# A two-layer gated cross-attention kernel: three instruction blocks are joined into one

## The chip, the cores and the metric

The kernel runs on one core of a Trainium2 chip. A core has five engines with an instruction stream each: TensorE (PE in the profile, with its weight loads as PEld), VectorE (DVE), ScalarE (ACT), GpSimd (POOL) and SyncE (SP), and 16 DMA engines that they share. Engines meet only through semaphores. The metric is the time of one execution in microseconds of device time, taken as the median of several runs.

## The reference, cut to what matters

```python
x = x + tanh(g_xattn[0]) * L0_xattn(layernorm(x), ctx)   # correlation attention: top 13 delays
x = x + tanh(g_ffn[0])   * L0_ffn(layernorm(x))          # 8 experts, 2 per token, and a shared one
x = x + tanh(g_xattn[1]) * L1_xattn(layernorm(x), ctx, mask)   # 16 heads over 77 keys
x = x + tanh(g_ffn[1])   * L1_ffn(layernorm(x))          # 32 experts, 4 per token, and a shared one
```

x has 4 x 1024 rows of 256 float32 numbers, ctx has 4 x 77 rows. In layer 0's feed-forward part each row goes to 2 of 8 experts; in layer 1's to 4 of 32. The products of layer 0 and of layer 1's attention are made of three matmuls each on values split into a high and a low part.

## The kernel before, in words

The 4096 rows of x stay in SBUF (`x`, 32 tiles of 128 rows, or 8 chunks of 4 tiles). The program is written by hand engine by engine: each engine has its own list of instructions with its own waits, and nothing reorders them. It comes in three blocks, one behind the other, and each holds a list for each of the five engines:

- **Folds** (first block, L307 to L675). The context is multiplied into the weights of both attentions (`wqk1` and `vwo1` are the folded weights of layer 1, two heads at a time, and SP stores them to `wqk_d` and `vwo_d`), layer 0's attention scores give the 13 delays, and the first chunk is normalised for the feed-forward part. Its last instructions are ACT's `fold_heads(7)` (L461), PE's transposes of chunk 0 (`transposes_job`, L225) and SP's stores of the last two heads (L334).
- **Layer 0** (second block, L842 to L1555). First the dense part: for each of 8 chunks the router, the shared expert and the attention of the chunks to come. Then 39 blocks of 256 rows that are gathered by expert: SP loads a block's rows (`rows<-slots_d`), PE, ACT and DVE compute, POOL scatters the result to `y0_d` with two indirect DMAs (L999). Beside them the folded weights of layer 1 are split into high and low parts and stored again. ACT opens the block with `wr_hi` (L1015) and the eviction of the transposed chunk 0 (`x_hi`, L1013); DVE follows with `x_lo` (L1153), and PE's first matmul there, the router of chunk 0 (L1399), needs that.
- **Layer 1** (third block, L1759 to L2331). SP first loads the two expert results of the first four tiles from `y0_d` (`first_rows`, L1765, into the end of `xbT`); DVE adds them to x and takes the statistics (`mv_a`), POOL makes 1/sqrt(var + eps) of them (`rstd`, L1834 to L1844), ACT normalises (`xa`, L1913), PE transposes, ACT and DVE evict (`xa_hi`, L1908, and `xa_lo`, L2024), and the first scores follow (L2191). From there on attention, routing and dispatch run as a pipeline over the 32 tiles, then the 32 experts, then the sums.

Between two blocks every engine runs a drain (it waits until what it has issued is done) and the five meet in a barrier: SP, ACT, DVE and PE report to POOL, and POOL releases them. In the profile these instructions carry the line of the block that they end: L307, L842 and L1759.

At the end of layer 0's list, POOL waits until all its scatters have landed, one semaphore for each of six groups of blocks (L1003 and L1004), and SP waits until the last parts of the split weights are stored and the cleared tables written (L918, L919). In layer 1's `first()`, POOL makes its constants (`xa`'s column of ones, `tri`, `allone`, `cum`, `rows`, `outrow`, `ones1`, `full`: L1847 to L1863); DVE and PE wait for all eight of them by the semaphore `c3` before `xa_lo` of tile 0 and before the first scores.

Of the kernel before, what the change touches and what calls it, by code (L numbers as in the profile page):

```python
# [7 lines left out]
ALU = mybir.AluOpType  # L8
ACT = mybir.ActivationFunctionType
AX = mybir.AxisListType  # L10
# [7 lines left out]
S = 77  # L18
# [82 lines left out]
def build(nc, io):  # L101
    root = ExitStack()
    with root:
# [143 lines left out]
        with one:  # L247
# [59 lines left out]
            with nc.Block() as block:  # L307
                @block.sync
                def _(sp):
                    def load_x(c):  # L310
                        sp.dma_start(x[:, c * CT:(c + 1) * CT, :], x_v[:, c * CT:(c + 1) * CT, :]).then_inc(x_in[c], 16)

                    def load_heads(m):

                        want(sp, f1_mm, 8 * (m - NH + 1))
                        cols = slice(m * P, (m + 1) * P)
                        for w, src in ((wk1, "wk1"), (wv1, "wv1")):
                            sp.dma_start(w[:, m % NH, :, :], io[src].rearrange("(k p) n -> p k n", p=P)[:, :, cols])\
                               .then_inc(w1_in[m % NH], 16)
                        for w, src in ((wqT1, "wqT1"), (wo1, "wo1")):  # L320
                            sp.dma_start(w[:, m % NH, :], io[src][cols, :]).then_inc(w1_in[m % NH], 16)

                    def store_heads(m):

                        sp.wait_ge(f1_out, 8 * m + 4)
                        if m == 0:
                            sp.wait_ge(mask_row, 64)
                        for b in range(B):
                            sp.dma_start(wqk_d[b].rearrange("(k p) n -> p k n", p=P)[:, :, 2 * m * S:2 * (m + 1) * S],
                                          wqk1[:, m % 2, :, b, :]).then_inc(qk1_stored[m % 2], 16)  # L330
                        sp.wait_ge(f1_out, 8 * m + 8)
                        for hh in range(2):
                            h = 2 * m + hh
                            sp.dma_start(vwo_d[:, h * S:(h + 1) * S, :].rearrange("b s n -> s b n"),  # L334
                                          vwo1[:, m % 2, hh, :, :]).then_inc(vo1_stored[m % 2], 16)

                    for name, dst in (("ctxT", ctxT), ("wk0", wk0), ("wqT0", wqT0)):
                        sp.dma_start(dst[:], io[name].rearrange("(k p) n -> p k n", p=P)).then_inc(w0_in, 16)
                    sp.dma_start(bias0[:], io["bias0"].rearrange("p (a k) -> p a k", a=3)).then_inc(w0_in, 16)
                    load_x(0)  # L340
                    load_x(1)
                    for name, dst in (("wv0", wv0), ("wo0", wo0)):
                        sp.dma_start(dst[:], io[name].rearrange("(k p) n -> p k n", p=P)).then_inc(bo_in, 16)
                    for c in range(2, CHUNKS):
                        load_x(c)
                    for b in range(B):
                        sp.dma_start(vwo0[S:S + 1, b, :], io["bo0"].rearrange("(a n) -> a n", a=1)).then_inc(bo_in, 16)
                    sp.dma_start(htab[:], io["htab"].rearrange("(c p) n -> p c n", p=P)).then_inc(htab_in, 16)
                    sp.dma_start(mask_u[:], io["mask"].rearrange("b s -> (b s)").rearrange("(a n) -> a n", a=1))\
                      .then_inc(mask_in, 16)  # L350
                    for m in range(NH):
                        load_heads(m)
                    sp.dma_start(wgu0[:], io["wgu0"].rearrange("(k p) n -> p k n", p=P)[:, :, E0 * 2 * P:])\
                      .then_inc(ffn0_w_in, 16)
                    sp.dma_start(wd0[:], io["wd0"].rearrange("(u p) n -> p u n", p=P)[:, E0:, :]).then_inc(ffn0_w_in, 16)
                    sp.dma_start(wr0[:], io["wr0"].rearrange("(k p) n -> p k n", p=P)).then_inc(ffn0_w_in, 16)
                    sp.wait_ge(mask_ready, 1)
                    for par in range(2):
                        for hh in range(2):
                            sp.dma_start(wqk1[P - 1:P, par, KD - 1, :, hh * S:(hh + 1) * S], mask_f[:]).then_inc(mask_row, 16)  # L360
                    for c in range(CHUNKS):

                        b, half = c // 2, c % 2
                        sp.wait_ge(s_out, c + 1)
                        for copy in range(2):
                            sp.dma_start(st_d[b, :, copy * L + half * CHUNK:copy * L + (half + 1) * CHUNK],
                                         sT[:, half, :]).then_inc(s_stored[half], 16)
                        if half:

                            for par in range(2):  # L370
                                sp.wait_ge(s_stored[par], 32 * (b + 1))
                            want(sp, uv_mm, b - 1)
                            for sign in range(2):
                                shift = bass.AP(st_d.tensor, b * S * 2 * L + (S - 1 if sign == 0 else L - S + 1),
                                                [[2 * L - 1 if sign == 0 else 2 * L + 1, S], [1, L]])
                                sp.dma_start(skew[:, b % 2, sign, :], shift).then_inc(skew_in[b % 2], 16)
                    for m in range(CHUNKS):
                        if m + NH < CHUNKS:
                            load_heads(m + NH)
                        store_heads(m)  # L380
                        if m == 2:
                            sp.wait_ge(w_ready, 2)
                            sp.dma_start(w_d, wrow[:]).then_inc(w_stored, 16)
                        if m == 3:
                            sp.wait_ge(mt_ones, 1)
                            sp.wait_ge(w_stored, 16)
                            shifted_job(sp, 0)
                            shifted_job(sp, 1)
                    sp.wait_ge(ffn0_w_in, 48)

                @block.gpsimd
                def _(pool):
                    pool.memset(ident[:], 0.0).then_inc(ident_zero, 1)
                    pool.memset(neghalf[:], -0.5).then_inc(consts_ready, 1)
                    pool.memset(signs[:, 0:3], 1.0).then_inc(consts_ready, 1)
                    pool.memset(signs[:, 3:4], -1.0).then_inc(consts_ready, 1)
                    pool.wait_ge(ident_zero, 1)
                    pool.affine_select(out=ident[:], in_=ident[:], compare_op=ALU.not_equal, fill=1.0, base=0,
                                       pattern=[[-1, P]], channel_multiplier=1).then_inc(ident_ready, 1)
                    pool.wait_ge(consts_ready, 3)  # L400

                    def last_column(m):

                        pool.wait_ge(w1_in[m % NH], 64 * (m // NH + 1))
                        pool.tensor_scalar(wqT1[:, m % NH, 0:D - 1], wqT1[:, m % NH, 0:D - 1], wqT1[:, m % NH, D - 1:D], None,  # L405
                                           ALU.subtract).then_inc(wq_ready, 1)

                    for c in range(CHUNKS):
                        ln_rstd_job(pool, c, c % 2)
                        if c == 1:  # L410
                            pool.wait_ge(mask_in, 16)
                            pool.tensor_scalar(mask_f[:].rearrange("p b s -> p (b s)"), mask_u[:], MASKED, None, ALU.mult)\
                                .then_inc(mask_ready, 1)
                    for m in range(CHUNKS):
                        last_column(m)
                        if m == CHUNKS - 2:
                            ln_rstd_job(pool, QB, 0)

                @block.scalar
                def _(act):  # L420
                    act.dma_start(gates[:, 0:2], bass.AP(io["g_xattn"].tensor, 0, [[0, P], [1, 2]])).then_inc(gates_in, 16)
                    act.dma_start(gates[:, 2:4], bass.AP(io["g_ffn"].tensor, 0, [[0, P], [1, 2]])).then_inc(gates_in, 16)
                    act.wait_ge(gates_in, 32)
                    act.activation(tg[:], gates[:], ACT.Tanh).then_inc(tg_ready, 1)
# [1959 lines left out]
```

## Time and profile before

| what | us |
|---|---|
| median of 3 runs | 1023.62 |
| lowest and highest run | 1015.46, 1024.27 |
| the profiled execution | 1024.65 |
| its span, first to last instruction | 1022.6 |

The profiled execution is 1.03 us above the median. Of its time 2.05 us lie outside the span. TensorE's granted clock was 0.926 of full speed on average. In the rows below times are microseconds from the span's start unless they are marked ns, and a name such as SPq or POOLq is an engine's sequencer: it shows instructions that don't reach the engine itself (waits, branches, drains, the issue of DMAs).

### The profile page before, as it was taken

What the parts mean: (1) busy time and instruction counts of PE and PEld (TensorE: products, weight loads), DVE (VectorE), ACT (ScalarE), POOL (GpSimd) and SP (SyncE); (2) the same over time, 40 slices, a digit from 0 to 9 for tenths busy, and PEclk for the clock granted to TensorE, in tenths of its full rate; (3) what the DMA queues carried; (4) which work ended last, traced back from release to release, by engine and by line L of the source; (5) the groups of instructions that cost most, each with busy time, mean ns of one, the idle gap of its engine ahead of it and who ended that gap; (6) DMA issues with size and microseconds to landing.
All of it is one profiled execution on the core that took longest, in us unless ns stands there. A gap on an engine that the chain in (4) does not pass through costs nothing. (4 is left out here: it accounts for less than half of the span.)

```text
span 1022.6 us, 18469 instructions
## 1 busy us (share of the span) xinstructions
PE 879.8 (86%) x5433; PEld 744.1 (73%) x5433; DVE 632.6 (62%) x2000; ACT 501.4 (49%) x1813; POOL 564.0 (55%) x635
## 2 busy tenths in 40 slices
PE   4998777999999979889199899999999978999940
PEld 3564446888888779889188889899898857888720
DVE  4603114688778857557278889999999843444441
ACT  1321654444544246546086778878878822222200
POOL 1400113466666727557448777767777653877851
PEclk8987997899999989999699999999999979999975
DMA  9630788367987888996499924514444205899687
GB/s 305 218 100 0 226 240 203 92 204 223 277 260 221 283 260 276 316 332 225 150 165 257 226 94 180 178 58 140 121 153 140 64 12 149 155 224 250 73 211 159
DMA packets 157812, 189.70 MB, mean 186 GB/s; under 512 B 16035, under 2 KB 137017, under 8 KB 157714
## 3 DMA queue, kind: packets, MB, share of 16 engines
q1 hardware_dynamic: 109810, 121.87, 39.9%
q0 software_dynamic: 30720, 46.46, 20.8%
q10 hardware_dynamic: 17184, 20.19, 5.8%
q8 instruction: 46, 0.75, 0.3%
q14 instruction: 52, 0.43, 0.1%
HBM read 96.19 MB, written 103.63 MB: 195 GB/s over the span
## 5 line engine op out<-in xcount | busy, mean ns | idle before, releaser
L1938 ACT ACTIVATE att<-bank,mx 128x77 f32<-128x77 f32 x512 | 159.0, 343 | 1.0 <-DVE mx L2019 0.9
L1879 POOL DMA_INDIRECT slots_d<-rows,place x128 | 131.4, 1027 | 36.4 <-issue 35.5
L1938 ACT ACTIVATION_READ_ACCUMULATOR att<-bank,mx 128x1 f32 x512 | 115.6, 226 | 0.0
L999 POOL DMA_INDIRECT y_d<-rows x78 | 77.3, 991 | 62.3 <-DVE rows L1377 34.7
L959 POOL DMA_INDIRECT slots_d<-rows,place x64 | 65.2, 1019 | 19.0 <-issue 19.0
L1399 PE MATMUL bank<-wd_hi,act_hi 128*128 128x256 f32 (+1 forms) x206 | 66.5, 323 | 1.3 <-DVE act_lo L1372 0.7
L1893 POOL DMA_INDIRECT acc_d<-expert_out,target_rows x32 | 49.6, 1550 | 26.8 <-issue 23.1
L953 POOL TENSOR_TENSOR act_lo<-prod,act_hi 128x512 fp32r<-128x512 f32 x28 | 36.8, 1313 | 39.9 <-ACT act_hi L1035 39.8
L2019 DVE TENSOR_REDUCE mx<-bank 128x6 f32<-128x462 f32 (+1 forms) x96 | 55.1, 573 | 5.6 <-PE bank L2193 4.9
L1401 PE MATMUL bank<-wd_hi,act_lo 128*128 128x256 f32 (+1 forms) x206 | 58.4, 284 | 0.0
L1400 PE MATMUL bank<-wd_lo,act_hi 128*128 128x256 f32 (+1 forms) x206 | 58.3, 283 | 0.0
L1893 POOL DMA_INDIRECT result<-expert_out,target_rows x32 | 49.5, 1546 | 14.3 <-issue 8.5
L2034 DVE TENSOR_TENSOR attT_lo<-bank,attT_hi 128x512 fp32r<-128x512 f32 (+2 forms) x128 | 55.6, 475 | 1.3 <-ACT attT_hi L1928 0.7
L1399 PE MATMUL bank<-x_hi,first_scores 128*128 128x512 f32 x128 | 53.3, 416 | 0.0
L2046 DVE TENSOR_TENSOR att<-att,den 128x924 f32<-128x924 f32 x64 | 51.2, 800 | 2.2
L1400 PE MATMUL bank<-x_lo,first_scores 128*128 128x512 f32 x128 | 52.0, 406 | 0.0
L1401 PE MATMUL bank<-x_hi,first_scores 128*128 128x512 f32 x128 | 52.0, 406 | 0.0
L1925 ACT ACTIVATE attT_hi<-bank 128x512 fp32r<-128x512 f32 x64 | 38.8, 608 | 25.4 <-PE bank L2230 25.4
L2230 PE MATMUL bank<-ident,att 128*128 128x128 f32 x320 | 51.0, 274 | 0.0
L405 POOL TENSOR_SCALAR wqT<-wqT 128x255 f32<-128x255 f32 x8 | 7.5, 941 | 78.0 <-DMA wo<-in_wo 77.9
L1399 PE MATMUL bank<-wgu_hi,x_hi 128*128 x156 | 48.1, 308 | 1.7 <-issue 1.7
L1979 ACT ACTIVATE expert_silu<-bank 128x256 f32<-128x256 f32 x32 | 12.3, 383 | 73.4 <-PE bank L2307 73.4
(318 smaller groups left out, 3009.9 us busy)
## 6 DMA issues: line engine op xcount, KB each, us to landing
rows<-slots_d SPq DMA_DIRECT2D x39, 260.0 KB, 4.3
slots_d<-zrow SPq DMA_DIRECT2D x8, 1168.0 KB, 10.8
expert_rows<-slots_d SPq DMA_DIRECT2D x32, 292.0 KB, 3.7
expert_gate_up<-in_wgu SPq DMA_DIRECT2D x28, 256.0 KB, 4.1
x_res<-y_d POOLq DMA_DIRECT2D x14, 512.0 KB
wqk_d<-wqk SPq DMA_DIRECT2D x32, 154.0 KB, 3.5
vwo_d<-vwo SPq DMA_DIRECT2D x16, 308.0 KB
x_res<-in_x SPq DMA_DIRECT2D x8, 512.0 KB, 8.5
```

What stands on the lines that cost most here:

```text
L959: pool.indirect_dma_start(slots0_d, bass.IndirectOffsetOnAxis(ap=place0[:, c % 3, i:i + 1], axis=0), rows_of(c)[:, i, :], None, bounds_che ...
L999: pool.indirect_dma_start(y0_d, bass.IndirectOffsetOnAxis(ap=x_rows(s)[:, b, D:D + 1].bitcast(I32), axis=0), y_rows(s, b), None, bounds_ch ...
L1399: pe.matmul(to, a_hi, b_hi, start=start, stop=False)
L1400: pe.matmul(to, a_hi, b_lo, start=False, stop=False)
L1401: return pe.matmul(to, a_lo, b_hi, start=False, stop=stop)
L1879: pool.indirect_dma_start(slots_d, bass.IndirectOffsetOnAxis(ap=place[:, n % 3, k:k + 1], axis=0), rows[:, n % 3, :], None, bounds_check=S ...
L1893: pool.indirect_dma_start(total, bass.IndirectOffsetOnAxis(ap=target[:, e % NY, b:b + 1], axis=0), y[:, e % NY, b, :], None, bounds_check= ...
L1938: last = act.activation(att[:, par, h * S:(h + 1) * S], bank[:, a, i * S:(i + 1) * S], ACT.Exp, scale=-1.0, bias=mx[:, par, h:h + 1], accu ...
L2019: dve.tensor_reduce(mx[:, par, h:h + count], e, AX.X, ALU.min).then_inc(mx_ready, 1)
L2034: last = dve.tensor_tensor(attT_lo[0:p1, cols], bank[0:p1, 3 + g % 2, at:at + w * P], attT_hi[0:p1, cols].bitcast(F32), ALU.subtract)
L2046: return dve.tensor_tensor(heads, heads, over, ALU.mult)
L2230: last = pe.transpose(bank[0:w, 3 + g % 2, (j % 4) * P:(j % 4 + 1) * P], att[:, par, j * P:j * P + w], ident[:])
```

## The change

The lists of the first two blocks become functions (`folds_sync`, `layer0_sync`, `folds_gpsimd` and so on), and each engine's list in the third block calls the two of its own before its old content. There is one block instead of three, so the two drains and barriers in between are gone. No instruction of an engine is reordered but for one: in POOL's `first()`, the norm of tile 0 (`rstd("a", 0, 0)`) comes behind the constants. And one wait is added: at the end of layer 0, SP waits for the six scatter semaphores itself, as POOL does.

```diff
-            with nc.Block() as block:
-                @block.sync
-                def _(sp):
+            def folds_sync(sp):
...
-                @block.gpsimd
-                def _(pool):
+            def folds_gpsimd(pool):
...
-            with nc.Block() as block:
-                @block.sync
-                def _(sp):
+            def layer0_sync(sp):
...
+                for g in range(6):
+                    sp.wait_ge(scattered[g], scat_end[g])
                 for par in range(2):
                     sp.wait_ge(part_out[par], POUT + 32 * dmas(PIECES - 2 + par))
                 sp.wait_ge(cleared, 16 * (2 * CHUNKS + 1 + E0))
...
                 @block.sync
                 def _(sp):
+                    folds_sync(sp)
+                    layer0_sync(sp)
+
                     y0_v = y0_d.rearrange("(n p k) d -> p n k d", p=P, k=K0)
...
                     def first():
                         pool.memset(xa[:, :, D - 1:D], 1.0).then_inc(c3, 1)
-                        rstd("a", 0, 0)
                         pool.memset(tri[:], 1.0).then_inc(c3_zero, 1)
...
                         pool.affine_select(out=tri[:], in_=tri[:], compare_op=ALU.not_equal, fill=float(CHOSEN), base=0,
                                            pattern=[[1, P]], channel_multiplier=-1).then_inc(c3, 1)
+                        rstd("a", 0, 0)
```

The same two calls are put at the head of the lists of POOL, ACT, DVE and PE.

At the first joint, ACT's list before, from the last folded heads to the first evictions of layer 0:

```order
L461 ACTIVATE vwo<-bank,tanh_gates 77x512 [waits fold1_mm] x4
L307 UNCONDITIONAL_BRANCH
L1006 UNCONDITIONAL_BRANCH [waits barrier_Pool_Activation_PE_DVE_SP_release]
L1015 ACTIVATE wr_hi<-wr 128x20
L1013 ACTIVATE x_hi<-bank 128x512 [waits ln_T]
L1013 ACTIVATE x_hi<-bank 128x512
```

And now:

```order
L457 ACTIVATE vwo<-bank,tanh_gates 77x512 [waits fold1_mm] x4
L1007 ACTIVATE wr_hi<-wr 128x20
L1005 ACTIVATE x_hi<-bank 128x512 [waits ln_T]
L1005 ACTIVATE x_hi<-bank 128x512
```

The wait for the barrier is gone; what is left is the wait for PE's transposes (`ln_T`).

At the second joint, SP's list before, from the last part of the split weights (`wd<-vwo_d`) to the first loads of layer 1:

```order
L853 DMA wd<-vwo_d 80x256
L842 UNCONDITIONAL_BRANCH [waits cleared,s_stored1,s_stored0]
L1760 UNCONDITIONAL_BRANCH [waits barrier_Pool_Activation_PE_DVE_SP_release]
L1765 DMA xbT<-y_d 128x512 x4
L1770 DMA even_values<-vwo_hi_d 128x9x256
```

And now (`s_stored0` and `s_stored1` are the semaphores of the stored parts; `rows_moved0` to `rows_moved3`, `experts_added0` and `experts_added1` are those of the scatters):

```order
L845 DMA wd<-vwo_d 80x256
L1758 DMA xbT<-y_d 128x512 [waits experts_added1,experts_added0,s_stored0,rows_moved3,s_stored1,rows_moved2,cleared,rows_moved1,rows_moved0]
L1758 DMA xbT<-y_d 128x512 x3
L1763 DMA even_values<-vwo_hi_d 128x9x256
```

The first load waits for the scatters themselves and no longer for POOL's release.

POOL's list at the same joint, before:

```order
L842 UNCONDITIONAL_BRANCH [waits rows_moved3,experts_added0,rows_moved2,experts_added1,rows_moved1,rows_moved0]
L1822 UNCONDITIONAL_BRANCH [waits barrier_Pool_Activation_PE_DVE_SP_gather]
L1847 MEMSET xa 128x2
L1837 TENSOR_SCALAR veps_a<-mv_a 128x1 [waits a_stats]
L1839 TENSOR_TENSOR rstd_a<-veps_a,neghalf 128x1 [waits a_eps]
L1843 TENSOR_SCALAR shift_a<-rstd_a,mv_a 128x1 [waits z_ready]
L1849 MEMSET tri 128x128
...
L1862 AFFINE_SELECT tri<-tri 128x128 [waits consts3_zero]
L1837 TENSOR_SCALAR veps_a<-mv_a 128x1 [waits a_stats]
```

And now:

```order
L1843 MEMSET xa 128x2 [waits rows_moved3,experts_added0,rows_moved2,experts_added1,rows_moved1,rows_moved0]
L1844 MEMSET tri 128x128
...
L1857 AFFINE_SELECT tri<-tri 128x128 [waits consts3_zero]
L1833 TENSOR_SCALAR veps_a<-mv_a 128x1 [waits a_stats]
L1835 TENSOR_TENSOR rstd_a<-veps_a,neghalf 128x1 [waits a_eps]
L1839 TENSOR_SCALAR shift_a<-rstd_a,mv_a 128x1 [waits z_ready]
L1833 TENSOR_SCALAR veps_a<-mv_a 128x1 [waits a_stats]
```

The constants stand ahead of the wait for the first statistics, and the norms of tiles 0 and 1 follow each other.

## Rows read from the trace of the kernel before

**Rows 1.** The page's first line.
```profile
span 1022.6 us, 18469 instructions
```

**Rows 2.** Timeline, first joint: start, length, engine, line, instruction, idle before.
```profile
153.04 2.65 ACT L461 ACTIVATE vwo<-bank,tanh_gates 77x512 f32<-77x512 f32 x4 [1.44 <-PE bank L624]
...
155.72 0.77 SPq L334 DMA_DIRECT2D vwo_d<-vwo  x2
...
156.98 0.22 ACT L1015 ACTIVATE wr_hi<-wr 128x20 fp32r<-128x20 f32 x1 [1.29 <-PEq L307]
...
158.21 1.29 DVE L1153 TENSOR_TENSOR x_lo<-bank,x_hi 128x512 fp32r<-128x512 f32 x2 [0.79 <-ACT x_hi L1013]
...
159.64 0.34 PE L1399 MATMUL bank<-wr_hi,x_hi 128*128 128x10 f32 x1 [4.22 <-DVE x_lo L1153]
```

**Rows 3.** Line L307: ns min/median/max, first and last start.
```profile
L307 POOLq DRAIN x1: 2137/2137/2137, 143.8 to 143.8; - x1
...
L307 ACTq EVENT_SEMAPHORE  x1: 17/17/17, 156.9 to 156.9; - x1
```

**Rows 4.** Windows: us, busy time (instructions) by engine, PE clock, DMA share, GB/s.
```profile
160.00:162.00 2.00, 2.00 (x11) 2.00 (x11) 2.00 (x1) 1.98 (x2) 1.00 (x1) 0.50 0.35 86
...
168.00:170.00 2.00, 1.15 (x7) 0.67 (x5) 1.17 (x4) 0.48 (x3) 0.00 (x0) 1.00 1.17 237
...
208.00:234.00 26.00, 25.65 (x157) 22.05 (x157) 20.78 (x67) 13.20 (x25) 17.95 (x18) 1.00 0.68 212
...
312.00:338.00 26.00, 24.71 (x162) 21.51 (x160) 20.25 (x74) 10.87 (x19) 19.53 (x19) 1.00 0.86 254
```

**Rows 5.** Waits of PE from 330 to 495: total us, times, longest.
```profile
PE bank L1506 <- DMA rows<-slots_d: 10.0, 4, 4.8
```

**Rows 6.** Lines L1004 and L842, the second joint on the sequencers.
```profile
L1004 POOLq EVENT_SEMAPHORE  x3: 17/43/5492, 491.0 to 491.1; - x3
...
L842 SPq COMPARE_BRANCH  x1: 41/41/41, 490.5 to 490.5; - x1
...
L842 POOLq COMPARE_BRANCH  x1: 41/41/41, 496.7 to 496.7; - x1
L842 POOLq DRAIN  x1: 3823/3823/3823, 496.8 to 496.8; - x1
L842 SPq EVENT_SEMAPHORE  x1: 17/17/17, 500.8 to 500.8; - x1
```

**Rows 7.** Timeline behind the second joint.
```profile
500.92 1.76 SPq L1765 DMA_DIRECT2D xbT<-y_d  x4
...
506.22 0.31 POOL L1837 TENSOR_SCALAR veps_a<-mv_a 128x1 f32<-128x1 f32 x1 [5.21 <-DVE mv_a L2011]
...
507.65 0.20 POOL L1849 MEMSET tri<- 128x128 bf16 x1
...
509.12 0.38 ACT L1908 ACTIVATE xa_hi<-bank 128x256 fp32r<-128x256 f32 x1 [0.78 <-PE bank L2199]
...
509.55 0.29 POOL L1862 TENSOR_SCALAR_AFFINE_SELECT tri<-tri 128x128 bf16<-128x128 bf16 x1
509.88 0.42 DVE L2024 TENSOR_TENSOR xa_lo<-bank,xa_hi 128x256 fp32r<-128x256 f32 x1 [2.30 <-POOL tri L1862]
```

**Rows 8.** Line L1759, POOL's drain at the program's end.
```profile
L1759 POOLq COMPARE_BRANCH  x1: 46/46/46, 1018.3 to 1018.3; - x1
L1759 POOLq DRAIN  x1: 3902/3902/3902, 1018.5 to 1018.5; - x1
```

**Rows 9.** Timeline, POOL's last DMA and its last operation in the folds.
```profile
144.85 1.00 POOL L405 TENSOR_SCALAR wqT<-wqT 128x255 f32<-128x255 f32 x1
...
1003.26 0.86 POOL L1900 DMA_DIRECT2D result<-x_res  x1 [0.27 <-DVE x_res L2183]
```

**Rows 10.** Timeline of POOL in layer 1: arithmetic behind an indirect DMA.
```profile
546.61 0.97 POOL L1879 DMA_INDIRECT slots_d<-rows,place  x1 [0.30 <-issue]
547.61 0.27 POOL L1837 TENSOR_SCALAR veps_a<-mv_a 128x1 f32<-128x1 f32 x1
```

More of the change, by code:

```diff
@@ L675, in _, with scores @@
-                    transposes_job(pe, 0)
+                        last.then_inc(vwo_mm, 1)
+                pe.wait_ge(ident_ready, 1)
+                pe.wait_ge(consts_ready, 3)
+                def scores(c):
+                    pe.wait_ge(ln_xT, 2 * c + 2)
+                    want(pe, s_out, c)
+                    for k in range(KD):
+                        last = pe.matmul(bank[0:S, 2, :], wqk0[:, k, (c // 2) * S:(c // 2 + 1) * S],
+                                         xnT[:, c % 2, k, :], start=k == 0, stop=k == KD - 1)
+                    last.then_inc(s_mm, 1)
@@ new lines, in keys_values @@
+                def keys_values(m):
+                    pe.wait_ge(w1_in[m % NH], 64 * (m // NH + 1))
+                    for n, (w, done) in enumerate(((wk1, k1_out), (wv1, v1_out))):
+                        want(pe, done, m)
+                        for k in range(KD):
+                            last = pe.matmul(bank[:, 4 + n, 0:BS], w[:, m % NH, k, :], ctxT[:, k, :],
+                                             start=k == 0, stop=k == KD - 1)
+                        last.then_inc(kv1_mm, 1)
@@ new lines, in delay_sums @@
+                def delay_sums(b):
+                    pe.wait_ge(skew_in[b % 2], 32 * (b // 2 + 1))
+                    for c in range(8):
+                        for sign in range(2):
+                            last = pe.matmul(bank[:, 3, (b * 8 + c) * 2:(b * 8 + c) * 2 + 2],
+                                             skew[:, b % 2, sign, c * P:(c + 1) * P],
+                                             signs[0:S, 2 * sign:2 * sign + 2], start=sign == 0, stop=sign == 1)
+                    last.then_inc(uv_mm, 1)
@@ new lines, in correlation @@
+                def correlation():
+                    pe.wait_ge(uv_out, 2)
+                    pe.wait_ge(htab_in, 16)
+                    pe.wait_ge(s_out, CHUNKS)
+                    for c in range(8):
+                        pe.matmul(bank[0:B, 2, :], difV[:, c, :], htab[:, c, :], start=c == 0, stop=c == 7)
+                    pe.wait_ge(ln_xT, 2 * CHUNKS)
+                    for c in range(8):
+                        last = pe.transpose(bank[0:B, c // 4, (c % 4) * P:(c % 4 + 1) * P], sumU[:, c, :], ident[:])
+                    last.then_inc(h_mm, 1)
@@ new lines, in folds_tensor @@
+                ln_transpose_job(pe, 0, 0)
+                pe.wait_ge(fold_out, 3)
+                for c in range(CHUNKS):
+                    if c + 1 < CHUNKS:
+                        ln_transpose_job(pe, c + 1, (c + 1) % 2)
+                    scores(c)
+                    if c == 0:
+                        first_values()
+                    if c == 1:
+                        first_outputs()
+                    if c % 2 and c > 2:
+                        delay_sums((c - 3) // 2)
+                pe.wait_ge(vwo_out, B)
@@ L681, in build @@
+                keys_values(0)
+                delay_sums(B - 1)
+                keys_values(1)
+                correlation()
+                for m in range(CHUNKS):
+                    if 0 < m and m + 1 < CHUNKS:
+                        keys_values(m + 1)
+                    fold_heads(m)
+                    if m == 5:
+                        pe.wait_ge(vwo_out, B + 1)
+                        attention_job(pe, 0)
+                transposes_job(pe, 0)
         between = root.enter_context(ExitStack())
@@ L1904, in _ @@
                 def _(act):
+                    folds_scalar(act)
+                    layer0_scalar(act)
                     def evict_a(n, par):
```

1852 lines of the change are left out of this document (896 added, 956 removed).

## The prediction, made before the changed kernel was run

> **What bounds the kernel now.** The page comes first: the span is 1022.6 us [rows 1]. A change that takes two barriers away and moves one norm has its price at the two joints, so these are read and not the shares of busy time. I read each joint in the timeline, in all engines at once, and ask which engine arrived last, what it was doing, and who restarts last behind it. Then come the sequencers' own instructions at the block lines, which are not in the timeline: they tell a wait from a drain.
>
> First joint. ACT's last fold ends at 153.04 + 2.65 = 155.69, and PE's last transposes ended at 159.64 - 4.22 = 155.42 [rows 2]. SP is the last to arrive: it issues its last two stores until 155.72 + 0.77 = 156.49, and the release reaches ACT at 156.9 [rows 2, 3]. ACT's first instruction of layer 0 starts at 156.98, and from it hangs PE's restart, through `x_hi` and DVE's `x_lo` (158.21), at 159.64. So 156.98 - 155.69 = 1.29 us of ACT's idle time lie on the path, and SP's stores, which held it, are needed by nobody there.
>
> Second joint. POOL is the last. Its wait for the scatters is 5.49 us long and ends at 491.1 + 5.49 = 496.6; it leaves the list at 496.7. SP has been at the joint since 490.5. Then the reader should see one row: POOL's drain, from 496.8, takes 3.82 us [rows 6]. Only then come the barrier and SP's release at 500.8, and SP issues the loads of layer 1's first rows at 500.92 [rows 6, 7]. All of layer 1 stands behind these loads: DVE adds them to x, takes the statistics, and POOL makes `rstd` at 506.22. So from 496.6 on nothing that layer 1 needs is missing.
>
> A drain is not always dear. POOL's own at the first joint is recorded from 143.8 with 2.14 us, thus to 145.94, and POOL's last operation there ran to 144.85 + 1.00 = 145.85 [rows 3, 9]: 0.09 us behind it. POOL had issued no DMA until then. At the program's end it had, and the drain there takes 3.90 us, though POOL's last DMA was issued at 1003.26 and its wait for all of them was over at 1018.3 [rows 8, 9]. So the price of some 3.8 us belongs to the drain itself after POOL has issued DMAs, not to work that is still under way.
>
> **The change part by part.**
>
> - *First joint.* The drain and the barrier go; ACT's `wr_hi` follows the last fold at 155.7. Gain 1.3 us, as ACT's own idle row says. POOL's constants of layer 0 move ahead by more, for POOL stood idle from 145.85; nobody waits for them: worth nothing. SP's next DMAs wait for its own stores and don't move. Does the 1.3 us reach the end? PE is busy 25.65 of 26 us in the first of the five windows from 208 to 338, and 24.71 in the last [rows 4], so the dense part moves as a whole. In the 39 blocks PE waits 10.0 us for loaded rows, in four waits [rows 5]; those loads follow the dense part's scatters and the blocks' own progress, not a fixed time. I take the whole 1.3 us; the ends are 0 (the loads of the blocks eat it) and 1.3.
> - *Second joint.* SP waits for the scatters itself. The semaphore that came last did so at 496.6; POOL needed 0.1 us more for the others, and SP issues about 0.1 us after a release (500.8 to 500.92). So the loads go out at 496.8 in place of 500.92: gain 4.1 us. The added wait holds up nothing in SP's list that did not stand behind the barrier before. The lower end is what the barrier alone is worth if the drain turns into something else: 500.92 less 500.6, 0.3 us.
> - *Constants ahead of the first norm.* They run from 507.65 to 509.55 + 0.29 = 509.84, 2.2 us, plus a column of ones of 0.1 us [rows 7]. DVE's `xa_lo` starts at 509.88, as the last of them ends, though ACT's `xa_hi` was there at 509.12 + 0.38 = 509.50. With a hand-over of 0.04 us (509.84 to 509.88) to 0.1 us, 0.3 us are on the path. Moved ahead, the constants begin when POOL's wait ends, at 496.7, and are done at 499.0; the statistics come 4.1 us earlier than before, at 502.1. That is 3.1 us of cover. Gain 0.3 us. If the cover were gone, the first norm would come up to 2.3 us late. POOL's next work, the norm of tile 1 and the first two adding DMAs, comes earlier by the 2.2 us as well, but PE is not waiting for it: worth nothing.
>
> Sum: 1.3 + 4.1 + 0.3 = 5.7 us, from the profiled execution's 1024.65 to 1019.0. That execution is 1.03 us above the median of 1023.62, so a median of **1017.9 us**, 0.6% less. By the bounds the sum is 0.3 to 5.7 us, without the clock (below).
>
> One rule of the Trainium skill speaks against the largest term. VectorE: DVE Perf Modes, section The DRAIN you can't avoid, says of the drains that surround a program that they are constant at about 12 ns on all five engines. By it two drains would be worth nothing, and the sum would be the one of the second rival. Here POOL's took 3823 and 3902 ns [rows 6, 8], so for POOL the trace does not agree.
>
> **The rivals.**
>
> 1. *PE's clock gives more.* PE's granted clock is 0.50, thus 1.2 GHz, when it restarts at the first joint after 4.22 us of idle time, and 1.00 again in the window from 168 [rows 2, 4]. The idle time becomes 2.9 us. If the clock then doesn't fall, or comes back sooner, up to half of the 159.64 to 168 us is saved, 4.2 us more: some 1014. For it: less idle time. Against: 2.9 us is still a long pause, and rows show none of that length there. 10%.
> 2. *A wait takes the drain's place.* If the 3.8 us are the landing of the last scatters, SP now waits as long itself, and only 0.3 us of barrier go: 1.3 + 0.3 + 0.3 = 1.9 us, 1021.7. For it: the drain stands right behind the DMAs. Against: the wait on the semaphores was over before the drain began, and the drain at the end is as long with all landed [rows 6, 8]. 6%.
> 3. *The drain's work moves to POOL's next instruction.* POOL would be free at 500.6, its constants done at 502.9, and the first norm 0.8 us late: 4.9 us, 1018.7. For it: a drain waits for something that the profile doesn't name. Against: arithmetic starts 0.03 us behind an indirect DMA [rows 10], and at the program's end POOL had issued nothing for 14 us. The skill's PSUM — Partial Sum Buffer, section Engine vs sequencer instructions, says that a drain waits until the engine is fully idle, which would be this rival. 5%.
> 4. *Slower: PE falls to the lower clock more often.* The place is the dense part, where new meetings of ACT, POOL and PE open pauses. Each stretch like the one from 159.64 to 168 costs up to 4.2 us; from the second one on, 8.4 us against 5.7, the change loses: 1026.3. For it: all of layer 0 is shifted against SP's stores. Against: PE has hardly a pause there [rows 4]. 3%.
> 5. *The runs' own spread.* One run of three lay at 1015.46, 8.2 us below the median, and the trace doesn't tell why. If the changed kernel's median falls there, it is 1009.8. 14%.
>
> **How the numbers follow.** The forecast has the other 62%, with 1016.5 to 1019.5 as its own range. From 1009 to 1022 the range holds rivals 1 to 3 and nearly all of the fifth. About 1%, 10.2 us, is what a measurement of this kernel can tell from no change. Faster than 1013.4 takes the fifth rival and a part of the first: 0.17. Slower than 1033.9 has no case but more than one of the fourth kind: 0.02. Within 1%: 0.81.
>
> **What the changed profile would show.** Right: no idle time of ACT ahead of `wr_hi`, PE's first router matmul some 2.9 us behind its transposes; no POOL drain but the one at the end, with its 3.9 us; SP's first load of `xbT` within 0.3 us of POOL's `xa` memset; `xa_lo` 0.1 us behind `xa_hi`, with POOL's `tri` long done. From there the distance to the end of the span as before, 1022.6 - 500.92 = 521.7 us less 0.3. Wrong: POOL's memset starts with the same 3.8 us behind the wait (rival 3); SP's wait ends only some 4 us behind POOL's last scatter (rival 2); the distance from PE's first router matmul to POOL's last scatter grows by the gain of the first joint (the blocks eat it); or the windows show the lower clock where it was not before (rival 4).

## The result, and the profile after

The changed kernel's median is **1008.67 us** (five runs, 1002.68 to 1011.46), against 1022.81 for the five runs of before: a ratio of 0.9873 with a 95% interval of 0.9830 to 0.9916, or 8.6 to 17.4 us less. The forecast was 1017.9, 0.6% less, with a range from 1009.0: the sign and the two places were right, the size was about half of what came, the median lies 0.3 us below the range, and the case "faster by over 1%" had been given 0.17. A second batch of six runs gave a ratio of 0.9890 (0.9846 to 0.9934); with it, the changed kernel's eleven runs have a mean of 1008.2 us, and 72 runs of before beside the experiments one of 1019.7: 11.5 us. Runs more than 1.5% above the quickest of their kernel, two of before and three in the experiments, two of these over 1900 us, are left out of all means.

The page after, its first line and the clock in 40 slices [rows 1]:

```profile
span 1000.3 us, 18447 instructions
...
PEclk8878997999999989999699999999999999999975
```

The profiled execution is the quickest of its five, and that of before (1024.65) was slower than each of its three runs. So a difference of the two spans (22.3 us) is more than the change gives, and a second profile of each kernel stands beside them below.

**First joint.** The timeline after (start, length, engine, line, instruction, idle before), which answers to [rows 2]:

```profile
147.79 2.40 ACT L457 ACTIVATE vwo<-bank,tanh_gates 77x512 f32<-77x512 f32 x4 [0.54 <-PE bank L618]
...
150.08 0.22 ACT L1007 ACTIVATE wr_hi<-wr 128x20 fp32r<-128x20 f32 x1
150.19 1.08 ACT L1005 ACTIVATE x_hi<-bank 128x512 fp32r<-128x512 f32 x2
150.22 0.77 SPq L332 DMA_DIRECT2D vwo_d<-vwo  x2
...
152.74 0.35 PE L1389 MATMUL bank<-wr_hi,x_hi 128*128 128x10 f32 x1 [3.09 <-DVE x_lo L1144]
```

ACT's `wr_hi` has no idle time ahead of it any more, SP's last stores are issued beside it and hold nobody, and PE restarts after 3.09 us in place of 4.22; 2.9 had been worked out.

**Second joint.** POOL's wait for the scatters, by line, and the timeline behind it [rows 6, 7]:

```profile
L997 POOLq EVENT_SEMAPHORE  x3: 17/43/4911, 478.8 to 479.0; - x3
```

```profile
483.93 1.76 SPq L1758 DMA_DIRECT2D xbT<-y_d  x4
483.96 0.10 POOL L1843 MEMSET xa<- 128x2 f32 x1 [1.24 <-issue]
...
485.90 0.29 POOL L1857 TENSOR_SCALAR_AFFINE_SELECT tri<-tri 128x128 bf16<-128x128 bf16 x1
...
488.30 0.31 POOL L1833 TENSOR_SCALAR veps_a<-mv_a 128x1 f32<-128x1 f32 x1 [2.10 <-DVE mv_a L2013]
...
491.20 0.38 ACT L1907 ACTIVATE xa_hi<-bank 128x256 fp32r<-128x256 f32 x1 [0.78 <-PE bank L2204]
...
491.68 0.42 DVE L2026 TENSOR_TENSOR xa_lo<-bank,xa_hi 128x256 fp32r<-128x256 f32 x1 [2.03 <-ACT xa_hi L1907]
...
492.25 0.72 PE L2196 MATMUL bank<-first_scores,xa_hi 128*128 128x462 f32 x1 [1.09 <-DVE xa_lo L2026]
```

POOL's wait began at about 479.0 and took 4.91, so it ended at 483.9; SP's first load goes out at 483.93 and POOL's memset at 483.96. The drain is gone and nothing has taken its place. `tri` is done at 486.19, 2.1 us ahead of the first norm's work, and `xa_lo` follows 0.10 us behind the end of `xa_hi`, as the prediction had it. The only drain that POOL has left at the end of a block is the one at the end of the program [rows 8]:

```profile
L1749 POOLq COMPARE_BRANCH  x1: 46/46/46, 995.9 to 995.9; - x1
L1749 POOLq DRAIN  x1: 3909/3909/3909, 996.1 to 996.1; - x1
```

**Stage by stage.** I cut both programs at five marks: PE's last transposes of the folds, its first router matmul, its `selb,tri` matmul at the end of the dense part, POOL's last scatter, and PE's first score of layer 1. Windows of after (span of the stage, busy time of the engines, PE's granted clock, DMA share, GB/s):

```profile
148.55:152.74 4.19, 1.10 (x11) 0.89 (x9) 1.47 (x3) 4.19 (x7) 0.00 (x0) 0.94 0.89 269
...
152.74:330.94 178.20, 171.80 (x1005) 147.09 (x1005) 131.70 (x451) 77.88 (x134) 109.43 (x109) 0.96 0.74 217
330.94:481.75 150.81, 133.03 (x1037) 126.39 (x1037) 99.89 (x225) 80.38 (x179) 88.79 (x91) 0.96 0.86 281
481.75:492.25 10.50, 0.69 (x2) 0.32 (x3) 3.23 (x9) 1.63 (x4) 6.56 (x19) 0.50 0.67 212
492.25:1000.30 508.05, 443.87 (x2814) 388.44 (x2814) 351.15 (x1175) 282.73 (x1383) 333.79 (x369) 0.96 0.63 153
```

The same of before:

```profile
154.33:159.64 5.31, 1.09 (x10) 0.88 (x9) 1.47 (x3) 3.92 (x6) 2.53 (x15) 0.79 0.57 175
...
159.64:338.58 178.94, 172.52 (x1004) 147.40 (x1005) 131.69 (x451) 77.89 (x134) 109.32 (x109) 0.96 0.74 215
338.58:494.49 155.91, 136.32 (x1037) 129.13 (x1037) 100.42 (x225) 80.55 (x179) 89.95 (x91) 0.94 0.84 272
494.49:510.44 15.95, 0.69 (x2) 0.32 (x3) 3.22 (x9) 0.98 (x2) 4.79 (x16) 0.50 0.54 165
510.44:1022.60 512.16, 448.10 (x2814) 391.90 (x2814) 350.97 (x1175) 283.48 (x1384) 336.11 (x371) 0.95 0.62 151
```

The reader is to compare the third number of each row, the stage's length, and its clock. In the table the second pair of profiles stands beside the first (us):

| stage | before, two profiles | after, two profiles | difference, pair 1 and pair 2 |
|---|---|---|---|
| folds, to PE's last transposes | 154.33, 150.20 | 148.55, 149.65 | -5.8, -0.6 |
| first joint, to the first router matmul | 5.31, 6.23 | 4.19, 4.19 | -1.1, -2.0 |
| dense part of layer 0 | 178.94, 179.85 | 178.20, 178.12 | -0.7, -1.7 |
| 39 blocks, to the last scatter | 155.91, 157.14 | 150.81, 154.83 | -5.1, -2.3 |
| second joint, to the first score | 15.95, 15.82 | 10.50, 10.52 | -5.5, -5.3 |
| layer 1 from the first score on | 512.16, 511.86 | 508.05, 510.09 | -4.1, -1.8 |
| sum | 1022.6, 1021.1 | 1000.3, 1007.4 | -22.3, -13.7 |

The two joints give 6.6 and 7.3 us, a little more than the 5.7 that were worked out. The rest lies in stages in which no instruction was changed, and there two profiles of one kernel differ by up to 4.1 us, nearly as much as the two kernels do. Even the folds, which end ahead of both joints, are 5.8 us shorter in the first pair. What of this rest belongs to the change was the question for the experiments. Outside the span the changed kernel gives 0.4 us back: time less span is 2.04 us on average before and 2.44 after.

### The profile page after: what moved, and what is told of

Its sections match the earlier page's. It is cut to its first block and busy times, and to the rows that moved or that the text cites. A ratio compares the mean times of both kernels' runs of the same rounds, so it can differ in the third digit from the quotient of the medians.

```text
span 1000.3 us, 18447 instructions
## 1 busy us (share of the span) xinstructions
PE 868.3 (87%) x5433; PEld 735.8 (74%) x5433; DVE 632.4 (63%) x2000; ACT 500.7 (50%) x1813; POOL 563.0 (56%) x635
```

## The experiments

All runs, each kernel beside runs of before on the same chip. The time at 1.2 GHz is twice (1 less the mean granted clock) times the span, averaged over the runs; idle time of PE at that clock is in it. Times are means; the ratio compares with the runs of before in the same batch, so it can differ a little from the ratio of the means.

| kernel | ratio to before (95%) | time (runs) | clock | us at 1.2 GHz |
|---|---|---|---|---|
| before | | 1019.7 (72) | 0.931 | 140 |
| changed, both batches | 0.9873 (0.9830 to 0.9916), 0.9890 (0.9846 to 0.9934) | 1008.2 (11) | 0.939 | 123 |
| constants alone | 1.0007 (0.9981 to 1.0033) | 1020.2 (12) | 0.930 | 143 |
| drain alone | 0.9986 (0.9962 to 1.0010) | 1018.3 (12) | 0.931 | 139 |
| first joint alone | 0.9938 (0.9914 to 0.9961) | 1014.9 (6) | 0.934 | 135 |
| second joint alone | 0.9932 (0.9906 to 0.9959) | 1012.6 (4) | 0.936 | 129 |
| drain put back | 0.9935 (0.9907 to 0.9964) | 1013.1 (12) | 0.935 | 131 |
| longer pause at the first joint | 0.9916 (0.9888 to 0.9945) | 1012.4 (11) | 0.936 | 130 |
| pauses filled in part | 0.9886 (0.9843 to 0.9929) | 1008.5 (6) | 0.944 | 112 |
| pauses filled | 0.9879 (0.9849 to 0.9910) | 1007.6 (6) | 0.946 | 109 |
| no drain at the end | 0.9857 (0.9824 to 0.9890) | 1005.7 (6) | 0.939 | 123 |
| both of the last two | 0.9878 (0.9841 to 0.9914) | 1006.7 (7) | 0.947 | 107 |

**The kernel before again.** No edit.

> The kernel before, unchanged, for its spread: each run's time beside its own mean granted clock, and a second profile. Theory A (the joints give the 5.7 us that were worked out; what the changed kernel has beyond it is PE's time at 1.2 GHz, which differs from run to run): the runs spread by some 8 us as the three of before do, the quicker ones have the higher mean clock, and at a clock of 0.935 to 0.940, where the changed kernel takes 1007 to 1011 us, this one takes some 6 us more, 1013 to 1017. Theory B (one joint is worth about 8 us more than was worked out, whatever the clock): at the same clock this one takes 14 us more, and its stages outside the joints are as long as those of the changed kernel.

Measured: 12 runs from 1016.77 to 1023.16, ratio 0.9997. The clock and the time do go together: over the 72 runs of before, a line through the spans rises by 0.34 us for each us at 1.2 GHz (correlation 0.77). At nearly the same clock the kernels still differ: the 14 runs of before with a mean clock of 0.935 to 0.941 have a mean of 1016.6 us, the seven of the changed kernel in that span (of both batches) 1008.5, so 8.1 us. The clocks of the two groups are not quite the same: 129 us at 1.2 GHz against 124, which by that line is worth some 1.7 of the 8.1 and leaves 6.4. Theory A had said 6, B 14. And the changed kernel has on average 17 us less at 1.2 GHz, which neither theory had a reason for.

**Each joint alone.** The changed lists, put into blocks in two other ways:

```
first joint alone:            second joint alone:
  Block: folds, layer 0         Block: folds
  Block: layer 1                Block: layer 0, layer 1
```

> The first joint alone taken away: folds and layer 0 in one block, a block of its own for layer 1, constants ahead of the first norm as in the change. Theory A: 1.3 + 0.3 = 1.6 us less than before by rows, POOL's drain of 3.8 us there at the second joint, and beyond it only what the clock does. Theory B1 (the first joint carries the rest, because PE's clock falls less often behind it): 8 to 10 us less than before, 1013 to 1015. Theory B2 (the second carries it): no more than 1.6 us.

> The second joint alone taken away: folds in a block of their own, layer 0 and layer 1 in one, constants ahead of the first norm. Theory A: 4.1 + 0.3 = 4.4 us less than before. Theory B1: no more than 4.4 us. Theory B2: 12 us less, 1010 to 1011.

Measured: 6.3 us less (4.0 to 8.8) and 6.9 us less (4.2 to 9.6). Together that is 13.2 us; by the means of the table it is 4.8 and 7.1, together 11.9. The changed kernel has 11.5 by its mean, so the joints add up within the spread. The second joint's 6.9 holds its expected 4.4 in the interval; the first joint's 6.3 does not hold its 1.6. By stages the first joint takes 3.90 us where it is gone and 6.20 where it is kept, the second 15.07 where kept and 10.54 where gone. B2 falls: the gain is not at the second joint alone. The first joint is worth more than the rows at it say; for the second that is not shown. The first joint's 6.3 lies between A's 1.6 and B1's 8 to 10, and since its interval reaches 8.8, B1 isn't excluded by these runs.

**The drain alone, at the second joint.**

```diff
-            with nc.Block() as block:
+            with nc.Block(no_gpsimd_drain=True) as block:     # layer 0's
```

> The kernel before with POOL's drain left out at the second joint and the barrier kept: three blocks, constants behind the first norm. Theory A: 3.8 us less than before, as the drain's row says; SP's first load some 0.6 us behind the end of POOL's wait for the scatters, in place of 4.3. Rival (the drain is only where POOL's own backlog is paid): POOL's first memset, or SP's release, comes as late as before, and the time doesn't change. Theory B2: 10 us or more.

Measured: 0.9986, 1.4 us less (3.9 less to 1.0 more). By line and in the timeline:

```profile
L842 POOLq EVENT_SEMAPHORE  x2: 17/17/17, 493.2 to 493.2; - x2
...
L842 POOLq COMPARE_BRANCH  x1: 41/41/41, 493.0 to 493.0; - x1
```

```profile
493.35 0.10 POOL L1847 MEMSET xa<- 128x2 f32 x1 [1.59 <-POOLq L842]
493.37 2.99 SPq L1765 DMA_DIRECT2D xbT<-y_d  x4
```

From POOL's branch out of its list to SP's first load it takes 0.4 us in place of 4.2 [rows 6, 7]: the drain's 3.8 us are gone from the joint, and nothing waits in its stead. Of these 3.8 us the second joint, 12.76 us long against 15.9, keeps 3.1, for the first rows' statistics come 5.68 us behind SP's first issue in place of 5.0. The runs can't tell 3.1 from their own spread: that the drain's 3.8 us were the price at this joint is read from the rows, and its worth in the time of the whole kernel is not shown by this run alone.

**The constants alone.** Three blocks as before, `rstd("a", 0, 0)` behind the constants and SP's wait for the scatters as in the change.

> Three blocks as before, with only the constants of layer 1 moved ahead of the first norm (and SP's waits for the scatters at the end of layer 0, which end while POOL waits for the same). By rows 0.3 us less than before: DVE's xa_lo comes 0.1 us behind ACT's xa_hi in place of 0.4 us. Theory C: no pause of PE changes, so its clock stays at 0.930 to 0.932 and the time at 1019.5 to 1020.5 us. Rival: the moved constants carry a part of what the two single joints gave beyond their rows (both had them): 2 us or more less than before.

Measured: 1.0007, within 0.3% either way. In the profile `xa_lo` starts 0.49 us behind the start of `xa_hi` in place of 0.76: the 0.3 us are there at their place. The rival, 2 us or more, is just outside the interval.

**The drain put back, but not in SP's way.**

```diff
                 for g in range(6):
                     pool.wait_ge(scattered[g], scat_end[g])
+                pool.drain()
```

> The changed kernel with one drain of POOL put back behind its wait for the scatters; SP no longer stands behind it. If the drain has a price of its own once POOL has issued DMAs: POOL's first memset of layer 1 starts some 4.1 us behind the end of its wait, the constants are done at some 490, rstd of the first tile comes 1.8 us late, and the time is 1.8 us above the changed kernel. Rival (the drain was long only since it stood ahead of a barrier, or waited for what SP's loads now wait for): the memset starts within 0.5 us and the time is that of the changed kernel.

By line, then in the timeline:

```profile
L998 POOLq DRAIN  x1: 3821/3821/3821, 488.4 to 488.4; - x1
```

```profile
488.44 1.76 SPq L1759 DMA_DIRECT2D xbT<-y_d  x4
...
492.34 0.10 POOL L1844 MEMSET xa<- 128x2 f32 x1 [5.11 <-issue]
...
492.58 0.18 DVE L2014 BATCH_NORM_AGGREGATE mv_a<-bst_a 128x2 f32<-128x6 f32 x1
...
494.28 0.29 POOL L1858 TENSOR_SCALAR_AFFINE_SELECT tri<-tri 128x128 bf16<-128x128 bf16 x1
494.66 0.24 POOL L1834 TENSOR_SCALAR veps_a<-mv_a 128x1 f32<-128x1 f32 x1
```

The drain has its 3.82 us here too, with no barrier behind it and with the scatters landed: SP's wait for them is over at 488.44, and the drain runs on to 492.3. It is a price of its own. The norm stands behind the constants at 494.66, and the second joint is 12.13 us long in place of 10.5, so 1.6 us, where 1.8 had been expected. The runs are 4.9 us longer than those of the changed kernel (1013.1 against 1008.2, with 2.1 to 7.8 as the interval), more than expected; where the other 3.3 lie the one profile doesn't tell, and the runs have 131 us at 1.2 GHz against 123.

**The changed kernel again.**

> The changed kernel again, for more runs with their mean granted clock and a second profile. The trace tells 1.2 GHz time (twice 1 less the mean clock, times the span): 17 us less of it in the five runs of the changed kernel than in 35 runs of the kernel before (123.9 against 141), and over the six profiles at hand the stretch from PE's first router matmul to POOL's last scatter is 0.44 us longer for each us of it. Theory C (the joints give the 5.7 us of the rows, and shorter pauses leave PE less often at 1.2 GHz, which gives the rest): mean clock again 0.936 to 0.940, time 1006 to 1010 us, and the stretch of layer 0 on the same line of 0.44. Theory D (the rest was luck of five runs): the clock falls back to 0.931 to 0.933 and the time to 1013 to 1016 us, 5.7 us below before.

Measured: 0.9890, mean clock 0.939 over the two batches: the gain is no luck of five runs, and theory D falls. Its stages are in the table above.

**A longer pause at the first joint, without a barrier.**

```diff
+                for spare in (kT0[:, 0, :], kT0[:, 1, :], vT0[:, 0, :], vT0[:, 1, :], wqk0[:, 0, :]):
+                    act.activation(spare, ctxT[:, 0, :], ACT.Copy)      # behind ACT's last fold
```

> The changed kernel with five copies of 128x308 put behind ACT's last fold, 0.35 us each by the fold's own rows, so that ACT, and through it PE's router matmul, comes 1.7 us later at the first joint; no barrier and no drain come back. PE's pause there is then some 4.8 us, as in the kernels with the joint (4.2 to 5.1), in place of 3.1. If the length of that pause is what leaves PE at 1.2 GHz more often in layer 0: the stretch from the router to the last scatter goes from some 331 to 335 us with 9 us more of low clock, and the time from 1008 to 1013 or 1014 us. If the pause isn't the cause: 1.7 us more, 1010 us, with the low clock of the changed kernel (some 123 us).

The restart of PE in the timeline, and two windows behind it, 30 us and the whole dense part:

```profile
158.09 0.35 PE L1391 MATMUL bank<-wr_hi,x_hi 128*128 128x10 f32 x1 [4.54 <-DVE x_lo L1146]
```

```profile
158.09:188.09 30.00, 26.52 (x102) 21.67 (x103) 14.29 (x54) 10.98 (x19) 7.74 (x7) 0.70 0.53 134
158.09:338.05 179.96, 173.56 (x1005) 148.08 (x1005) 131.68 (x451) 78.00 (x134) 109.33 (x109) 0.95 0.73 213
```

PE's pause is 4.54 us, the joint 5.65 us as in the kernels that keep it, and the time is 1012.4 us, 4.2 more than the changed kernel (1.0 to 7.4), with 130 us at 1.2 GHz against 123. Of the 4.2, 1.5 are the pause. The dense part, 179.96 us, is 2.1 us above the five profiles with the joint gone and nothing else done to PE (176.77 to 178.20, mean 177.8). So the longer pause is followed by a longer dense part at a lower clock, with no barrier and no drain near, in the one profile there is; what the runs lose beyond that, some 0.6 us, is within their spread.

**The pauses filled with transposes of the identity into a free bank.** First in part, then to the end:

```diff
                 transposes_job(pe, 0)
+                idle_transposes(pe, 25)        # 16 in the first version
...
+                        idle_transposes(pe, 126)       # 96
                         transpose_a(0, 0)
+                        idle_transposes(pe, 6)         # none
```

> The changed kernel with transposes of the identity into a free bank in PE's two pauses at the joints, 16 (2.2 us at 2.4 GHz) ahead of the first router matmul and 96 (13 us) ahead of layer 1's first transposes. Theory C says what the low clock behind a joint costs: if PE keeps 2.4 GHz, the 10.2 us at 1.2 GHz behind the first joint and the 4.8 us behind the first score of layer 1 go, at 0.44 us each 4.5 and 2.1 us, so up to 6.6 us below the changed kernel, some 1002 us. Rival E (the low clock behind a joint costs little, since PE waits there for others anyway): 0 to 2 us below. Rival F (the filling work brings the clock down elsewhere, or stands in the way of the router's matmuls): the same as the changed kernel or slower.

> As the kernel with the filled pauses, but filled to the end: 25 transposes at the first joint, 126 ahead of layer 1's first transposes and 6 behind them, 0.11 us each as they turned out there (they left 1.35 and 4.4 us open, and the clock fell behind both). If PE then keeps 2.4 GHz: the low clock behind the first joint (10.2 us, less up to 4.5 us of time) and behind the first score (3.8 us of it, 1.9 us of time) goes, and the time is 1002 to 1006 us. If the clock falls all the same, or what is won is waited for elsewhere: 1007 to 1009 us, as the changed kernel.

The first version left 1.35 and 4.40 us open, and PE's clock was at 1.2 GHz behind both; its time is that of the changed kernel, which tells nothing of the price. The second, in the timeline at the first joint and in two windows like those above:

```profile
150.41 2.89 PE L544 MATMUL bank<-ident 128*128 128x128 f32 x25
153.66 0.24 PE L1394 MATMUL bank<-wr_hi,x_hi 128*128 128x10 f32 x1 [0.36 <-DVE x_lo L1149]
```

```profile
153.66:183.66 30.00, 26.48 (x131) 22.06 (x132) 17.57 (x59) 11.95 (x20) 9.13 (x9) 0.89 0.58 149
153.66:328.95 175.29, 168.90 (x1004) 144.35 (x1005) 132.20 (x451) 77.89 (x134) 109.43 (x109) 0.98 0.74 221
```

In 30 us PE gets 131 matmuls done, against 102 behind the longer pause; the clock is 0.89 against 0.70, and the dense part is 2.5 us shorter than the changed kernel's 177.8. But the time hardly moves (0.9879; 1007.6 us against 1008.2, between 3.2 less and 2.0 more, so 2.5 us less would be near the edge of what these runs can tell). In the 39 blocks PE's waits for loaded rows are 12.1 us in this profile, against 7.9 and 9.7 in the two of the changed kernel. That these waits eat what the dense part wins is not shown: they are 11.3 and 11.7 us in two profiles without any filling (no drain at the end, longer pause), and the blocks, 154.25 us, are no longer than in the changed kernel's second profile (154.83). The waits of PE there, total, times, longest, as in [rows 5]:

```profile
PE bank L1501 <- DMA rows<-slots_d: 12.1, 2, 6.3
```

**No drain at the end**, and with it the filled pauses:

```diff
-            with nc.Block() as block:
+            with nc.Block(no_gpsimd_drain=True) as block:     # the only block
```

> The changed kernel with POOL's drain left out at the end of its one block. If the 3.9 us of the drain there lie on the path as at the second joint: some 3.9 us less, 1004 us. Rival (the end of the program waits for the same thing in another place): 1008 us, and a row at the end as long as the drain was.

```profile
L1749 POOLq EVENT_SEMAPHORE  x2: 17/17/17, 1003.7 to 1003.8; - x2
...
L1749 POOLq COMPARE_BRANCH  x1: 46/46/46, 1003.5 to 1003.5; - x1
```

From POOL's branch to the end of the program it takes 0.3 us in place of 4.3, no other row has grown at the end, and layer 1 is 504.74 us long, 3.3 below the shortest profile that has the drain. The median is 1006.14, 1.4% below before (1.1% to 1.8%). It beats before; that it beats the changed kernel too (1005.7 against 1008.2 us in the means) is likely by the rows, but not shown: the two ratios' intervals overlap over most of their length.

> Both joints gone, PE's two pauses filled with 25, 126 and 6 transposes, and no drain of POOL at the end of the block. If the two parts add: the 2 to 4 us of the end drain (runs of the changed kernel without it have a mean of 1005.7 against 1008.2 us) and the 0.6 us of the filled pauses (1007.6): some 1004 to 1005 us. If what the kept clock wins in the dense part (2.9 us from the router's first matmul to the 1.9 us pause in the one profile of it) reached the end: 1002. In the profile, the dense part is expected at 175 us again, in place of 178, and PE's waits for loaded rows in the blocks longer by as much if the blocks' loads eat it.

Measured: 1006.14, mean 1006.7. The dense part is 175.28 us again, the blocks took 158.12 with 11.6 us of waits for rows. The filling adds nothing that the runs show: the two parts were expected to add up to 1004 or 1005 us.

## Why the prediction was right in its places and short in its sum

- **First joint, +1.3.** The mechanism held; measured are 1.7, the mean of five profiles that keep the joint (5.31 to 6.23, mean 5.79) less the 4.1 of those without it. The term was a little small: in the one profile at hand the joint was shorter than in the other four.
- **The step behind it failed:** "the dense part moves as a whole". It doesn't keep its length. The windows that it rested on begin at 208 us [rows 4]; of the 48 us from the router's first matmul to there, which hold PE's pauses of 0.9 and 2.6 us, the rows show only four, and "PE has hardly a pause there" in the fourth rival leaves them out too. Ordered by PE's pause ahead of it:

| PE's pause at the first joint | profiles | length of the dense part, us |
|---|---|---|
| 4.22 to 5.13 (joint kept) | 5 | 178.24 to 179.85, mean 179.0 |
| 4.54 (longer pause, joint gone) | 1 | 179.96 |
| 2.81 to 3.09 (joint gone) | 5 | 176.77 to 178.20, mean 177.8 |
| 1.35 (filled in part) | 1 | 177.86 |
| 0.36 (filled) | 2 | 175.28, 175.29 |

  So without the joint the dense part is 1.2 us shorter on average. The difference goes with PE's clock, but not where the first rival (10%, "some 1014") had put it. In the 10 us behind the router's first matmul the granted clock is 0.50 to 0.66 in the five profiles with the joint and 0.51 to 0.54 in the five without: what the rival would have saved there isn't saved. The difference lies 20 to 30 us behind that matmul, at the end of the pause of 2.6 us. The row of before, then that of after (10 us each; the granted clock is the third number from the end):

```profile
179.64:189.64 10.00, 9.41 (x37) 7.49 (x38) 5.57 (x17) 5.00 (x10) 2.02 (x2) 0.66 0.00 0
```

```profile
172.74:182.74 10.00, 8.62 (x40) 7.23 (x41) 5.97 (x17) 5.79 (x11) 2.54 (x2) 0.83 0.00 0
```

  The clock there is 0.66 in four of the five with the joint and behind the longer pause, 0.83 in the fifth and in four of the five without, 1.00 in the last. Over all 14 profiles the dense part's length follows its own time at 1.2 GHz: 0.41 us for each us, with a correlation of 0.99. The fifth with the joint (second joint alone) has a pause of 5.10 us at the joint and still 178.24 us, so the pause's length doesn't decide by itself; why the later fall is shorter without the joint stays open.
- **Second joint, +4.1 and +0.3.** The drain was the price (3.8 us in four places: two in before, one put back, one at the end of after), SP's wait added nothing, the second and third rivals fell. The rule of the Trainium skill that was held against this term (VectorE: DVE Perf Modes, section The DRAIN you can't avoid: about 12 ns on all engines) speaks of the drains ahead of and behind a program. It doesn't cover the four here: they are the kernel's own, three of them from its blocks and one from its list, and the one at the program's end went when the block was told to leave it out. The drains in the traces that are nearest to it, at the program's start in before, took 7 to 10 ns on four engines and 167 on POOL. But the joint shrank by 5.4 us, not 4.4: from SP's first issue to the first rows' statistics it is 4.1 us after, against 5.0 before (4.1 to 4.6 in all profiles without a barrier there). The prediction held that distance fixed. Why these loads land 0.9 us sooner is not settled; with a barrier ahead of them they took 4.4 to 5.7.
- **The lengths from there to the end were held fixed too**, "521.7 us less 0.3". They were 516.3 and 518.4 in the two profiles.
- **What the sum missed.** By the profiles the joints and the dense part come to 1.7 + 1.2 + 5.4 = 8.3 us, less 0.4 outside the span. The means of the runs differ by 11.5. Some 3.6 are left, in the 39 blocks and in layer 1. On average these are shorter by about that much, but the profiles of one program differ by more: the blocks took 150.8 to 157.3 us, mean 154.1, in the five profiles without the first joint and 154.5 to 157.3, mean 156.0, in the five with it; layer 1 took 508.1 to 511.3, mean 509.8, in seven without the second joint and 510.6 to 512.2, mean 511.6, in four with it (508.5 in the one that keeps the barrier but not the drain). The clock goes with it: the blocks have 16.4 us at 1.2 GHz without the first joint and 21.1 with it, and over the 14 profiles their length rises by 0.36 us for each us (correlation 0.74). The runs point the same way. Of their 17 us less at 1.2 GHz, some 5 are idle time of PE that no longer exists, and 12 at 0.34 us each would be 4.1, with the dense part's 1.2 in it; with the joints' 7.1, less 0.4, that makes 10.8 of the 11.5. That is an estimate from the runs and not shown by a run of its own: why the blocks and layer 1 should be less often at 1.2 GHz stays open. The fifth rival (the spread, 14%) has a share in it only in so far as one profile of each kernel could not show it.
- **Slower, 0.02:** nothing of it was seen.

## What to carry to other kernels

Price a block boundary by the row of POOL's drain once POOL has issued DMAs, and by the last arrival at the barrier; at the joints both came out as the rows said or a little larger. The drain at the program's very end can be left out the same way: its row went, but that this beats the changed kernel is not shown. And don't hold the stages behind a removed pause fixed: PE's clock falls in pauses here, and a pause of 4 to 5 us, against one of 3, went with its own difference and on average about another microsecond in the dense part behind it. Look for it by the granted clock at every pause of that part, and not only at the one that was removed. And before trusting a sum of 6 us, take a second profile of the kernel before: its untouched stages moved by 0.3 to 4.1 us from one execution to the next.

## What the runs showed of the hardware that was not expected

- A drain of POOL took 3.82 to 3.91 us in four places, whether the DMAs that it had issued had just landed or long before, and whether a barrier followed or not; so did all 17 such drains in the traces of all runs. The same instruction before any of POOL's DMAs ended 0.09 us behind its last operation [rows 3, 9]. No run separates the DMAs from the other work that POOL does only behind the folds (its IOTA instructions), so that the DMAs are the cause is argued.
- The same pause doesn't always bring PE's clock down as far. The 2.6 us pause in the dense part, which ends 18 to 22 us behind the router's first matmul, stands in all profiles, but the 30 us behind that matmul, which hold it, ran at 0.70 to 0.83 of the full clock, and at 0.89 only where the pause at the joint had shrunk to 0.36 us.
- PE kept at work on the identity stayed at 2.4 GHz through both joints (granted clock 1.00 in both, against 0.94 and 0.50 in the changed kernel). The dense part behind it was 2.5 us shorter, but the runs show no gain in the whole (1007.6 against 1008.2 us).
